# A two-block transformer: the query parts written to memory once, by chunk, and the query stack loaded by three transfers that repeat their rows

## The chip, the cores and the metric

One core of one Trainium2 chip runs the whole program in one launch. The metric is the device time of that launch in microseconds (us), smaller is better. TensorE (PE) multiplies matrices, VectorE (DVE) reduces and adds, ScalarE (ACT) applies functions and moves results out of PSUM, GpSimd (POOL) does side work, and SyncE (SP) issues nearly all transfers (DMAs) between the on-chip memory (SBUF) and the chip's main memory. 16 DMA engines carry them.

## The reference, cut to what matters

The input x has 2 sequences of 1024 tokens with 128 features. Four blocks follow, each on a layer norm of x and added to x: an attention with 16 heads of 8 features, a feed-forward net on values rounded to FP4, a stack of 6 transformer layers, and a last feed-forward net. The change lies in the attention, which runs once in the first block and once in each of the 6 layers:

```python
q = (h @ wq + bq_).reshape(Bx, Sx, H, HD).transpose(0, 2, 1, 3)      # H = 16, HD = 8, Sx = 1024
k = (h @ wk + bk_).reshape(Bx, Sx, H, HD).transpose(0, 2, 1, 3)
v = (h @ wv + bv_).reshape(Bx, Sx, H, HD).transpose(0, 2, 1, 3)
scores = jnp.einsum('bhqd,bhkd->bhqk', q, k) * scale
scores = scores * smask          # 6 layers: kept where the bits of q's and k's place do not meet
a = jax.nn.softmax(scores, axis=-1)
att = jnp.einsum('bhqk,bhkd->bhqd', a, v)
```

## The kernel before, in words

**Halves.** The work goes by halves: one sequence in one attention layer. The first attention has 2 halves (the dense stage, `A0`), the 6 layers have 12 (the sparse stage, `A1`). A half's queries and keys are 1024 tokens, in two chunks x = 0, 1 of 512.

**Stacks.** A head has only 8 features, so float32 accuracy is made by parts: a query value is split into three bf16 parts (high, middle, low), a key value too. The score is the sum over all 9 pairs of parts, done as one matmul with 72 rows (`R_PAIR` = 3 x 3 x 8). For that the queries stand in `QS` with each part i repeated for j = 0, 1, 2 (rows i, j, d), and the keys in `KS` with parts j inside each i. Ten rows of mask bits and three rows of a running maximum follow. ACT writes the high part into `PQ` or `PK` (L783), DVE or POOL make the middle and low parts, and the partition layout is changed from (d, head) to (part, d) rows through main memory: `write_parts` writes the parts of a chunk to `scq` (three copies, one for each j) and `sck` (one), `load_q` and `load_k` read stacks of 8 heads (s = 0 or 1) into `QS` and `KS`.

**Units.** A half is four units k = 0..3: head group s = k // 2, query chunk x = k % 2. Pass A (L659) makes scores with queries as weights, and DVE reduces them to the maximum of each query (L948). The maximum is split in three parts, transposed to `mt`, and `move_max` sends it with three small transfers (L1076) into three rows of `QS`. Pass B (L679) makes the scores again, keys as weights, with the maximum subtracted in the same matmul; ACT takes the exponential (L804) and PE multiplies by the values (L694). PE's first matmul of a unit in pass B waits for `m_loaded`, the landing of that unit's three rows.

**Order.** The place of every step on PE, ACT and DVE is written out by hand in slots (82 for a sparse half); pass B of a half runs from slot 36 into the next half's slot 35, beside that one's pass A. In a sparse half the units of pass A start at slots 10, 31, 49 and 70, those of pass B at slots 36, 63, 77 and 104. PE executes in that order and stops at the first wait that is not met.

**SP's queue.** SP issues in the order of `sp_half`, and also stops at the first wait. For a sparse half it is: `move_max` of the half before's unit 3; `load_q(1, 0)`; `move_max` 0; `load_k(1)`; `load_q(1, 1)`; `move_max` 1; for the next half `write_parts(0)`, the layer's weights where due, `write_parts(1)`, `load_q(0, 0)`; `move_max` 2; for the next half `load_k(0)`, `load_q(0, 1)`. ACT's queue carries the small transfers of the maxima of units 2 and 3 (`sce`, `emr`). A load waits until pass B of the half before has done with the part of the stack that it overwrites, and until the parts are written.

Of the kernel before, what the change touches and what calls it, by code (L numbers as in the profile page):

```python
# [6 lines left out]
BF16 = mybir.dt.bfloat16  # L7
# [5 lines left out]
P = 128  # L13
D = 128
B, S = 2, 1024
H, HD = 16, 8
NB = S // P
NT = B * NB
CH = 512
TC = CH // P  # L20
NC = NT // TC
CB = NC // B
VW = HD + 1
NP = 3
R_PAIR = NP * NP * HD
# [350 lines left out]
def build(nc, io):  # L376
    ctx = ExitStack()
    with ctx:
# [57 lines left out]

        pA, pB, pO, pG = psum("pA", ABANKS), psum("pB", BBANKS), psum("pO", OBANKS), psum("pG", 2)

        scq = nc.dram_tensor("scq", (B, NP, NP, P, S), BF16, kind="Internal").ap()
        sck = nc.dram_tensor("sck", (B, NP, P, S), BF16, kind="Internal").ap()  # L440
        sce = nc.dram_tensor("sce", (B, UNITS, P, MC), F32, kind="Internal").ap()

# [201 lines left out]
        def pe_half(pe, a, half, slots, ready):  # L644
            cur = a.alive(half)
            for u in range(slots):
                if cur and u in a.a_at:
                    n = a.a_at[u]
                    st = a.a[n]
                    if n == a.a_first[st.k] and st.k % 2 == 0:  # L650
                        half.wait(pe, a.stack[st.k // 2], 64, 64)
                    elif n == a.a_first[st.k]:
                        half.wait(pe, a.stack_x1[st.k // 2], 16, 16)
                    half.wait(pe, a.a_reduced, n + 1 - ABANKS, a.na)
                    for gg, r, (how, keys), at, width in st.parts:
                        for hd in range(NQ):
                            head = SH * (st.k // 2) + 2 * hd + gg
                            row = KS[0:R_A, head, :]
                            ins = pe.matmul(pA[QT * hd:QT * (hd + 1), a.a_bank(half, n), at:at + width],  # L659
                                            QS[0:R_A, r // NR, head, r % NR * QT:(r % NR + 1) * QT],  # L660
                                            row[:, keys * CH:(keys + 1) * CH] if how == "half"
                                            else allowed(row, 5, keys),
                                            start=True, stop=True, tile_position=(0, QT * hd), skip_group_check=True)
                    ins.then_inc(a.a_scored, 1)
# [38 lines left out]
        def act_job(act, a, half, name):  # L703
# [52 lines left out]
            elif kind == "v":  # L756
                hw(act, a.v_evac, x + 1, CB)
                for p in range(2):
                    src = VN[KT * p:KT * (p + 1), TC * x:TC * (x + 1), :]\
                        .rearrange("p t (r a d) -> p t r a d", a=2, d=HD)  # L760
                    for ab in range(2):
                        ins = act.activation(VDv[KT * ab:KT * (ab + 1), half.b, 2 * TC * x + p:2 * TC * (x + 1):2, :,
                                                 VW * ab:VW * ab + HD], src[:, :, :, ab, :], ACT.Copy)
                ins.then_inc(a.v_placed, 1)
            elif kind == "on":
                s, xh = divmod(x, 2)
                hw(act, a.ot_filled, x + 1, UNITS)
                act.activation(on_view(half, s, xh), ot_view(a.bank[f"ot{x}"]), ACT.Copy).then_inc(a.ot_read, 1)
            else:
                assert kind == "qk"  # L770
                k, z = n[1], 2 * x + n[1]
                src = pG[:, a.bank[name], :]
                hw(act, a.qk_filled, z + 1, 2 * CB)
                if half.off or x:
                    hw(act, a.qk_split, z - 1, 2 * CB)
                half_w = 48 if k == 0 else 16
                (half + -1).wait(act, (a.q_written, a.k_written)[k][x], half_w, half_w)
                scale = SCALE if k == 0 else 1.0
                bias = (bqs[:, 0:1] if k == 0 else cE[:, 1:2]) if a.sparse else 0.0
                if a.sparse and k == 0:  # L780
                    wait_layer(act, a.bqs, half, 1)
                act.activation(x32[:, k, :], src, ACT.Identity, scale=scale, bias=bias)
                act.activation((PQ, PK)[k][:, 0, x * CH:(x + 1) * CH], src, ACT.Identity, scale=scale, bias=bias)\  # L783
                    .then_inc(a.qk_evac, 1)
# [261 lines left out]

        def load_q(sp, a, half, s, x):
            (half + -1).wait(sp, a.b_scored, a.b_end[2 * s + x] + 1, a.nb)
            half.wait(sp, a.q_written[x], 48, 48)
            hs = slice(SH * s, SH * (s + 1))  # L1050
            q = scq[half.b].rearrange("i j (d h) t -> (i j d) h t", h=H)
            sp.dma_start(QS[0:R_PAIR, x, hs, :], q[:, hs, x * CH:(x + 1) * CH])\
                .then_inc((a.stack, a.stack_x1)[x][s], 16)

        def load_k(sp, a, half, s):
            (half + -1).wait(sp, a.b_scored, a.b_end[2 * s + 1] + 1, a.nb)
# [7 lines left out]
        def write_parts(sp, a, half, x):  # L1064
            b, ts = half.b, slice(x * CH, (x + 1) * CH)
            half.wait(sp, a.qk_split, 2 * x + 2, 2 * CB)
            for j in range(NP):
                sp.dma_start(scq[b, :, j, :, ts].rearrange("i p t -> p i t"), PQ[:, :, ts]).then_inc(a.q_written[x], 16)
            sp.dma_start(sck[b, :, :, ts].rearrange("j p t -> p j t"), PK[:, :, ts]).then_inc(a.k_written[x], 16)

        def move_max(sp, a, half, k):
# [631 lines left out]
```

## Time and profile before

| | us |
|---|---|
| median of 3 runs | 1875.08 |
| lowest, highest | 1864.85, 1877.22 |
| the profiled execution's own time | 1867.36 |
| its span (first to last instruction) | 1865.5 |
| PE busy | 1606.9 (86%) |
| DVE busy | 1392.1 (75%) |
| ACT busy | 1153.2 (62%) |
| POOL busy | 369.5 (20%) |
| packets of SP's transfers (q1), as a share of 16 engines' span | 27.4% |

A busy share is an average over stages. The dense stage runs to about 530 us, the sparse stage from about 597 to 1800 us. Engine names with a q (SPq, ACTq) are the sequencers, which issue transfers and wait. What an engine waited for is inferred from semaphores. "Issue" is idle time for which the profile shows no wait. A DMA share can be a little over 1, since a packet's time is counted from its start to its end and two can overlap.

### The profile page before, as it was taken

How to read it: one execution, taken by the hardware profiler on the slowest of the kernel's cores; microseconds unless marked ns; L12 is line 12 of the kernel's file. 1: busy time of each engine (PE TensorE's matmuls, PEld its weight loads, DVE VectorE, ACT ScalarE, POOL GpSimd, SP SyncE). 2: the span in 40 equal slices, each digit the busy share in tenths (PEclk: the TensorE clock that was granted, in tenths of full speed). 3: DMA queues.
4: the chain of work that ended last, by engine and by line, in shares of the span. 5: the costliest groups of instructions: out<-in, count | busy, mean ns of one | idle time of the engine just before them, and what ended most of it. 6: DMA issues, size and time to landing. Idle time of an engine off the chain costs nothing.

```text
span 1865.5 us, 66422 instructions
## 1 busy us (share of the span) xinstructions
PE 1606.9 (86%) x28545; PEld 905.1 (49%) x28545; DVE 1392.1 (75%) x3287; ACT 1153.2 (62%) x2046; POOL 369.5 (20%) x407
## 2 busy tenths in 40 slices
PE   2899998899866789898989889898989889888886
PEld 1233333233333355555656556566565656565553
DVE  6878889987678767776776858687777777767834
ACT  2157776677842376775666666767767667666732
POOL 2000000000011223232231313232313233222111
PEclk7569999999987699999999999999999999999988
DMA  8022102000004342425233333334233434342000
GB/s 168 13 53 83 41 3 53 2 3 12 17 11 128 104 113 56 112 55 150 55 110 69 114 79 92 80 106 95 77 90 92 114 76 103 93 107 49 6 7 17
DMA packets 153754, 130.79 MB, mean 70 GB/s; under 512 B 65029, under 2 KB 149445, under 8 KB 151445
## 3 DMA queue, kind: packets, MB, share of 16 engines
q1 hardware_dynamic: 136181, 125.75, 27.4%
q8 instruction: 225, 3.69, 0.8%
q10 hardware_dynamic: 17280, 0.79, 0.6%
q14 instruction: 68, 0.56, 0.1%
HBM read 79.25 MB, written 45.88 MB: 67 GB/s over the span
## 4 chain that ended last, share of the span: by engine, by line
PE 39%; DVE 11%; ACT 6%; issue 6%; DMA 2%; ACTq 1%; SPq 1%; POOL 0%; DVEq 0%
PE pB L679 8%; PE pO L694 7%; PE pA L659 6%; PE pG L628 5%; PE pG L638 5%; DVE mx L948 3%; ACT PB L804 3%; DMA QS<-mt 2%; DVE bst L479 1%; PE pG L572 1%; PE pG L514 1%; ACTq L1090 1%; PE pG L579 1%; ACT HT L717 1%; PE pA L1229 1%
## 5 line engine op out<-in xcount | busy, mean ns | idle before, releaser
L804 ACT ACTIVATE PB<-pB 128x512 f32<-128x512 f32 (+1 forms) x1496 | 832.1, 594 | 410.9 <-PE pB L679 373.0
L948 DVE TENSOR_REDUCE mx<-pA 128x1 f32<-128x512 f32 (+3 forms) x1000 | 645.0, 671 | 194.5 <-PE pA L659 192.0
L679 PE MATMUL pB<-QS,KS 85*32 85x256 bf16 (+3 forms) x11264 | 609.9, 284 | 60.0 <-ACT PB L804 35.6
L659 PE MATMUL pA<-KS,QS 82*32 82x256 bf16 (+2 forms) x8384 | 548.0, 312 | 83.5 <-DVE mx L948 33.8
L694 PE MATMUL pO<-PB,VD 128*32 128x128 f32 (+3 forms) x5632 | 465.9, 399 | 9.3 <-issue 6.2
L679 PEld LDWEIGHTS pB<-QS,KS 85*32 85x32 bf16 x11264 | 262.4, 96 | 346.4 <-ACT PB L804 239.7
L659 PEld LDWEIGHTS pA<-KS,QS 82*32 82x32 bf16 x8384 | 217.4, 98 | 289.8 <-DVE mx L948 113.1
L502 POOL TENSOR_TENSOR rstd<-vareps,mhalf 128x4 f32<-128x4 f32 x68 | 69.9, 1027 | 1003.0 <-DVE vareps L488 1001.9
L948 DVE TENSOR_REDUCE mxb<-pA 128x1 f32<-128x512 f32 x304 | 207.0, 681 | 10.9 <-PE pA L659 10.9
L694 PEld LDWEIGHTS pO<-PB,VD 128*32 128x32 f32 x5632 | 168.5, 112 | 43.2 <-issue 11.3
L628 PE MATMUL pG<-HT,wL 128*128 128x512 f32 x192 | 99.7, 646 | 33.0 <-ACT HT L717 30.7
L638 PE MATMUL pG<-wL,FF 128*128 128x128 f32 x768 | 91.7, 278 | 1.2 <-ACT FF L738 1.2
L638 PEld LDWEIGHTS pG<-wL,FF 128*128 128x128 f32 x768 | 87.5, 192 | 6.2 <-ACT FF L738 4.0
L738 ACT ACTIVATE FF<-pG,cL 128x512 f32<-128x512 f32 x96 | 66.0, 687 | 24.8 <-PE pG L628 23.0
L861 DVE TENSOR_TENSOR ON<-ON,pG 128x288 f32<-128x288 f32 x48 | 20.7, 449 | 78.6 <-PE pG L605 78.6
L628 PEld LDWEIGHTS pG<-HT,wL 128*128 128x128 f32 x192 | 34.4, 199 | 84.6 <-issue 47.4
L572 PE MATMUL pG<-HT,wE 128*128 128x512 f32 x112 | 68.3, 698 | 3.4 <-DVE VN L838 1.9
L514 PE MATMUL pG<-ident,N 128*128 128x128 f32 x320 | 55.1, 298 | 16.4 <-DMA rE<-in_b 8.9
L1026 POOL TENSOR_TENSOR VU<-VN 128x512 f32<-128x512 f32 x12 | 15.3, 1277 | 270.3 <-PE pG L592 270.2
L495 DVE TENSOR_SCALAR N<-N,mv,rstd 128x128 f32<-128x128 f32 x208 | 58.0, 342 | 13.6 <-POOL rstd L502 13.5
L717 ACT ACTIVATE HT<-pG 128x512 f32<-128x512 f32 x32 | 19.0, 595 | 62.4 <-PE pG L514 62.4
L514 PEld LDWEIGHTS pG<-ident,N 128*128 128x128 f32 x320 | 38.0, 150 | 36.7 <-DVE N L495 12.5
(195 smaller groups left out, 1534.9 us busy)
## 6 DMA issues: line engine op xcount, KB each, us to landing
scq<-PQ SPq DMA_DIRECT2D x84, 384.0 KB, 3.5
QS<-scq SPq DMA_DIRECT2D x56, 576.0 KB
KS<-sck SPq DMA_DIRECT2D x84, 384.0 KB
sck<-PK SPq DMA_DIRECT2D x28, 384.0 KB, 4.4
wL<-in_wL SPq DMA_DIRECT2D x6, 576.0 KB, 5.0
QS<-mt SPq DMA_DIRECT2D x168, 8.0 KB, 2.5
rE<-in_rE SPq DMA_DIRECT2D x7, 256.0 KB, 11.7
emr<-sce SPq DMA_DIRECT2D x96, 4.0 KB, 1.7
```

Source lines behind the costliest of these rows:

```text
L495: ins = v.tensor_scalar(dst[:, t, :], src[:, t, :], mv[:, t, 0:1], rstd[:, t:t + 1], ALU.subtract, ALU.mult)
L502: g.tensor_tensor(rstd[:, a], vareps[:, a], mhalf[:, a], ALU.pow).then_inc(ln.rs, 1)
L514: ins = pe.transpose(pG[:, bank, i * P:(i + 1) * P], src[:, TC * c + i, :], ident[:, :])
L572: pe.matmul(pG[:, bank, :], wE[:, n[1], :], HT[:, c * CH:(c + 1) * CH], start=True, stop=True)\
L628: pe.matmul(pG[:, bank, :], wL[:, D + n[1] * P:D + (n[1] + 1) * P], HT[:, c * CH:(c + 1) * CH], start=True, stop=True).then_inc(F1.filled, 1)
L638: ins = pe.matmul(pG[:, bank, i * P:(i + 1) * P], FF[:, x, k, i * P:(i + 1) * P], wL[:, D + HID + k * D:D + HID + (k + 1) * D], start=(k = ...
L659: ins = pe.matmul(pA[QT * hd:QT * (hd + 1), a.a_bank(half, n), at:at + width], QS[0:R_A, r // NR, head, r % NR * QT:(r % NR + 1) * QT], ro ...
L679: ins = pe.matmul(pB[32 * i:32 * (i + 1), a.b_bank(h, v), at:at + width], KS[0:R_B, head, k0:k0 + 32], allowed(QS[0:R_B, x, head, :], 3, k ...
L694: ins = pe.matmul(allowed(pO[32 * j:32 * j + 32, k % OBANKS, :], 3, kt & 7 if a.sparse else 0), VD[:, col:col + 32], PB[:, a.ring(bank)[0] ...
L738: act.activation(FF[:, x, m, :], pG[:, a.bank[name], :], ACT.Gelu, bias=cL[:, 2 + m:3 + m])\
L804: act.activation(PB[:, pos_, 0:st.cols], pB[:, a.b_bank(h, v), 0:st.cols], ACT.Exp).then_inc(a.b_exped, 1)
L948: v.tensor_reduce(dst[:, gs[0]:gs[-1] + 1, tl[0]:tl[-1] + 1:step], pA[:, a.a_bank(half, n), 0:len(gs) * len(tl) * st.width] .rearrange("p ...
```

## The change

The scratch tensor `scq` is laid out by sequence, part, chunk, and then 128 partitions x 512 tokens, with no copies for j. `write_parts` writes it with one transfer of 384 KB for each chunk in place of three. `load_q` issues three transfers, one for each part i, of 24 rows (j, d) of 4096 contiguous values (8 heads x 512 tokens, 8 KB) in place of one of 72 rows with 8 pieces of 1 KB each. The source of such a transfer is 8 rows (d), read three times by a leading dimension of step 0 (j). What PE, and ACT before it overwrites `PQ`, wait for follows the new number of transfers.

```diff
--- before.py
+++ after.py
@@ -436,7 +436,7 @@
 
         pA, pB, pO, pG = psum("pA", ABANKS), psum("pB", BBANKS), psum("pO", OBANKS), psum("pG", 2)
 
-        scq = nc.dram_tensor("scq", (B, NP, NP, P, S), BF16, kind="Internal").ap()
+        scq = nc.dram_tensor("scq", (B, NP, CB, P, CH), BF16, kind="Internal").ap()
         sck = nc.dram_tensor("sck", (B, NP, P, S), BF16, kind="Internal").ap()
         sce = nc.dram_tensor("sce", (B, UNITS, P, MC), F32, kind="Internal").ap()
 
@@ -648,9 +648,9 @@
                     n = a.a_at[u]
                     st = a.a[n]
                     if n == a.a_first[st.k] and st.k % 2 == 0:
-                        half.wait(pe, a.stack[st.k // 2], 64, 64)
+                        half.wait(pe, a.stack[st.k // 2], 96, 96)
                     elif n == a.a_first[st.k]:
-                        half.wait(pe, a.stack_x1[st.k // 2], 16, 16)
+                        half.wait(pe, a.stack_x1[st.k // 2], 48, 48)
                     half.wait(pe, a.a_reduced, n + 1 - ABANKS, a.na)
                     for gg, r, (how, keys), at, width in st.parts:
                         for hd in range(NQ):
@@ -773,8 +773,7 @@
                 hw(act, a.qk_filled, z + 1, 2 * CB)
                 if half.off or x:
                     hw(act, a.qk_split, z - 1, 2 * CB)
-                half_w = 48 if k == 0 else 16
-                (half + -1).wait(act, (a.q_written, a.k_written)[k][x], half_w, half_w)
+                (half + -1).wait(act, (a.q_written, a.k_written)[k][x], 16, 16)
                 scale = SCALE if k == 0 else 1.0
                 bias = (bqs[:, 0:1] if k == 0 else cE[:, 1:2]) if a.sparse else 0.0
                 if a.sparse and k == 0:
@@ -1046,11 +1045,13 @@
 
         def load_q(sp, a, half, s, x):
             (half + -1).wait(sp, a.b_scored, a.b_end[2 * s + x] + 1, a.nb)
-            half.wait(sp, a.q_written[x], 48, 48)
+            half.wait(sp, a.q_written[x], 16, 16)
             hs = slice(SH * s, SH * (s + 1))
-            q = scq[half.b].rearrange("i j (d h) t -> (i j d) h t", h=H)
-            sp.dma_start(QS[0:R_PAIR, x, hs, :], q[:, hs, x * CH:(x + 1) * CH])\
-                .then_inc((a.stack, a.stack_x1)[x][s], 16)
+            for i in range(NP):
+                q = scq[half.b, i, x].rearrange("(d h) t -> d (h t)", h=H)[:, SH * s * CH:SH * (s + 1) * CH]
+                sp.dma_start(QS[i * NP * HD:(i + 1) * NP * HD, x, hs, :].rearrange("p h t -> p (h t)"),
+                             q.unsqueeze(0).to_broadcast([NP, HD, SH * CH]))\
+                    .then_inc((a.stack, a.stack_x1)[x][s], 16)
 
         def load_k(sp, a, half, s):
             (half + -1).wait(sp, a.b_scored, a.b_end[2 * s + 1] + 1, a.nb)
@@ -1064,8 +1065,7 @@
         def write_parts(sp, a, half, x):
             b, ts = half.b, slice(x * CH, (x + 1) * CH)
             half.wait(sp, a.qk_split, 2 * x + 2, 2 * CB)
-            for j in range(NP):
-                sp.dma_start(scq[b, :, j, :, ts].rearrange("i p t -> p i t"), PQ[:, :, ts]).then_inc(a.q_written[x], 16)
+            sp.dma_start(scq[b, :, x].rearrange("i p t -> p i t"), PQ[:, :, ts]).then_inc(a.q_written[x], 16)
             sp.dma_start(sck[b, :, :, ts].rearrange("j p t -> p j t"), PK[:, :, ts]).then_inc(a.k_written[x], 16)
 
         def move_max(sp, a, half, k):
```

SP's queue, from `write_parts(0)` for the next half to the `move_max` of unit 3, for a half that loads no weights (`scq`, `sck`: scratch in main memory; `mt`: the maxima). Before:

```order
L1068 DMA scq<-PQ 128x3x512 x3
L1069 DMA sck<-PK 128x3x512
L1068 DMA scq<-PQ 128x3x512 x3
L1069 DMA sck<-PK 128x3x512
L1052 DMA QS<-scq 72x8x512
L1076 DMA QS<-mt 1x128x32 x3
L1062 DMA KS<-sck 24x8192 x3
L1052 DMA QS<-scq 72x8x512
L1076 DMA QS<-mt 1x128x32 x3
```

And with the change:

```order
L1068 DMA scq<-PQ 128x3x512
L1069 DMA sck<-PK 128x3x512
L1068 DMA scq<-PQ 128x3x512
L1069 DMA sck<-PK 128x3x512
L1052 DMA QS<-scq 24x1x4096 x3
L1076 DMA QS<-mt 1x128x32 x3
L1063 DMA KS<-sck 24x8192 x3
L1052 DMA QS<-scq 24x1x4096 x3
L1076 DMA QS<-mt 1x128x32 x3
```

Nothing changes places: two of three writes are gone, and a load of a query stack is three transfers. The order of instructions on PE, ACT, DVE and POOL is as before.

## Rows read from the trace of the kernel before

**Rows 1.** Page, part 1 and part 4: busy time, and the chain that ended last

```profile
PE 1606.9 (86%) x28545; PEld 905.1 (49%) x28545; DVE 1392.1 (75%) x3287; ACT 1153.2 (62%) x2046; POOL 369.5 (20%) x407
...
PE 39%; DVE 11%; ACT 6%; issue 6%; DMA 2%; ACTq 1%; SPq 1%; POOL 0%; DVEq 0%
```

**Rows 2.** Waits: engine, line, what it waited for: us in total, times, longest

```profile
PEld pB L679 <- DMA QS<-mt: 8.9, 11, 1.6
...
PE pA L659 <- DMA KS<-sck: 21.9, 1, 21.9
```

**Rows 3.** Page, part 6: transfers by tile, count, KB each, us from issue to landing

```profile
scq<-PQ SPq DMA_DIRECT2D x84, 384.0 KB, 3.5
QS<-scq SPq DMA_DIRECT2D x56, 576.0 KB
...
sck<-PK SPq DMA_DIRECT2D x28, 384.0 KB, 4.4
...
QS<-mt SPq DMA_DIRECT2D x168, 8.0 KB, 2.5
```

**Rows 4.** Timeline of SP, 1349 to 1393 us: start, duration, line, transfer, count

```profile
1349.32 2.35 SPq L1068 DMA_DIRECT2D scq<-PQ  x3
1351.71 0.59 SPq L1069 DMA_DIRECT2D sck<-PK  x1
1352.40 0.87 SPq L1052 DMA_DIRECT2D QS<-scq  x1
1354.87 2.30 SPq L1076 DMA_DIRECT2D QS<-mt  x3
1358.83 1.14 SPq L1062 DMA_DIRECT2D KS<-sck  x3
1360.07 0.31 SPq L1052 DMA_DIRECT2D QS<-scq  x1
1365.41 1.77 SPq L1076 DMA_DIRECT2D QS<-mt  x3
1380.38 0.31 SPq L1052 DMA_DIRECT2D QS<-scq  x1
1392.32 1.91 SPq L1076 DMA_DIRECT2D QS<-mt  x2
```

**Rows 5.** DMA view of 1349 to 1361 us: busy tenths and GB/s, 40 slices

```profile
DMA  0020899619999999999886788889898330079225
GB/s 0 0 55 0 307 365 369 215 48 365 355 386 379 389 386 379 379 369 297 215 205 215 242 210 181 217 177 184 171 155 125 55 80 24 11 165 328 55 109 164
```

**Rows 6.** Timeline of PE where unit 2 of pass B begins, in two halves

```profile
1358.79 0.40 PE L659 MATMUL pA<-KS,QS 82*32 82x128 bf16 x16
1360.55 0.40 PE L679 MATMUL pB<-QS,KS 85*32 85x512 bf16 x4 [1.37 <-DMA QS<-mt]
...
970.95 0.24 PE L659 MATMUL pA<-KS,QS 82*32 82x128 bf16 x3 [2.03 <-issue]
...
971.67 0.74 PE L679 MATMUL pB<-QS,KS 85*32 85x512 bf16 x4
```

**Rows 7.** Timeline of PE where unit 3 of pass B begins, same halves

```profile
993.87 0.43 PE L679 MATMUL pB<-QS,KS 85*32 85x512 bf16 x4
...
1380.58 0.43 PE L679 MATMUL pB<-QS,KS 85*32 85x512 bf16 x4
```

**Rows 8.** Windows: stretch, its length, busy of five engines, PEclk, DMA share, GB/s

```profile
995.00:997.00 2.00, 2.00 (x66) 1.60 (x57) 1.73 (x4) 1.46 (x4) 1.15 (x1) 1.00 0.75 225
213.00:217.00 4.00, 3.87 (x56) 1.28 (x48) 2.50 (x5) 2.56 (x5) 0.00 (x0) 1.00 0.82 180
1113.50:1118.50 5.00, 4.89 (x18) 1.98 (x19) 0.12 (x1) 4.21 (x6) 0.99 (x1) 1.00 0.72 164
...
1352.00:1354.00 2.00, 1.91 (x19) 1.06 (x16) 1.83 (x8) 1.03 (x3) 1.51 (x4) 1.00 1.08 378
971.40:974.80 3.40, 3.40 (x88) 2.96 (x81) 2.13 (x4) 1.57 (x3) 0.00 (x0) 0.50 0.72 164
1360.50:1363.90 3.40, 3.16 (x104) 2.02 (x104) 2.41 (x6) 2.76 (x6) 0.03 (x1) 1.00 0.81 183
```

**Rows 9.** Timeline of SP in the first 60 us

```profile
22.89 1.50 SPq L1068 DMA_DIRECT2D scq<-PQ  x3
24.43 0.81 SPq L1069 DMA_DIRECT2D sck<-PK  x1
28.89 0.34 SPq L1052 DMA_DIRECT2D QS<-scq  x1
...
38.43 1.13 SPq L1062 DMA_DIRECT2D KS<-sck  x3
```

**Rows 10.** Page, part 3: DMA queue, packets, MB, share of 16 engines

```profile
q1 hardware_dynamic: 136181, 125.75, 27.4%
q8 instruction: 225, 3.69, 0.8%
```

## The prediction, made before the changed kernel ran

> **What bounds the kernel now.** I read the page's busy times first, then the chain that ended last, then the waits by engine, then SP's timeline over one sparse half, and last the DMA view of the congested stretch in it. PE is busy 86% of the span and holds most of the chain, while DMA has only 2% of it [rows 1]. The reader is to see that bytes are not the limit: SP's queue takes 27.4% of the 16 engines' time [rows 10]. So what the change does to bytes is worth little by itself. It counts only where PE waits for a landing. The waits name two such places: `mt`, the maxima that pass B needs (8.9 us in 11 waits of weight loads), and one wait of 21.9 us for the key stack at the start [rows 2].
>
> The place to look at is therefore unit 2 of pass B, once in each sparse half that still has a next half: 11 times. [Rows 4] show SP there: at 1349.3 the writes of the second chunk, at 1352.4 the load of a query stack, at 1354.9 the three `mt` transfers that PE needs, all in one queue. [Rows 5] show the DMA engines working without a break from 1350.2 (fifth slice of 0.3 us) to about 1359.2. PE ends the work before at 1359.2 and starts unit 2 at 1360.55, 1.37 us late, waiting for `mt` [rows 6]. An `mt` transfer with nothing ahead of it lands in about 2.5 us [rows 3]; here 5.7 us pass from issue to use. So the tiny transfer waits behind the large ones.
>
> **The writes.** Two of three writes of 384 KB go, once for each chunk of 14 halves: 56 issues and 22.0 MB of 125.75 [rows 3, 10]. For the first chunk nobody waits. For the second chunk, 4 x 384 KB (three of `scq`, one of `sck`) stand ahead of the query load; at 378 GB/s [rows 8] one takes 1.04 us, so removing two frees the queue 2.1 us earlier. SP has about 1 us less to issue there (0.5 us each [rows 9]) and 0.8 us more for the two extra loads (0.38 us each, as the key loads [rows 4]); it then waits for the maxima anyway.
>
> **The query loads.** The bytes stay at 576 KB (589,824 B), in pieces of 8 KB in place of 1 KB. The question is how many of the 16 DMA engines carry them. In [rows 8] the window with a 72-row query load alone has a DMA share of 0.75, and those with 24-row key loads alone 0.82 and 0.72, where four full-height writes give 1.08, which is all 16. Twelve of 16 is 0.75, and 12 is the largest number up to 16 that divides both 72 and 24. So a transfer is dealt out by equal parts of its outermost dimension. The new query load has 24 rows as destination, but its source's outermost dimension is the 3 repeats. A part must be the same elements on both sides, and only 3 divides both. No row shows a transfer whose two sides differ in this way, so the bounds are 3 and 12 engines. I take 3, since a share in twelfths would cut a repeat of the source. And the three transfers take the same three engines: of the key loads three are out together [rows 4], and their share stays at 12 of 16.
>
> The Trainium skill says the same as a rule, and against this change: "DMA: Bandwidth & Descriptors", in the section on why a DMA increments its semaphore by 16, has the engine count as the largest number up to 16 that divides the slowest dimension of both sides, and its rules for kernel authors say that a leading zero-stride broadcast of c copies confines the whole DMA to at most c engines. By it they are the lowest-numbered three for each transfer.
>
> **The rate of one engine.** Full writes give 378 / 16 = 23.6 GB/s each [rows 8]. Key loads give only 164 / 12 = 13.7 to 180 / 12 = 15.0 [rows 8]. These are the ends. I take 23.6: the key loads put 12 engines on 24 rows, while three engines on 24 rows have eight rows each, and a query load over 72 rows already reaches 225 / 12 = 18.8, so it is the crowding on few rows that slows the keys. Three engines then carry 70.9 GB/s and a query load takes 8.3 us. At 13.7 it takes 14.3 us.
>
> The Trainium skill's page "SBUF — State Buffer" (section on the DMA port swizzle) gives four neighbouring partitions one port of 27.2 GB/s. By it 24 rows have six ports, 163 GB/s, which the 164 GB/s of the key loads agree with, and three engines on two ports each would not be held by them.
>
> **The sum for one half.** In the half of [rows 4 to 6]: bytes start at 1350.2; two writes, 0.79 MB at 378 GB/s, take 2.1 us: 1352.3. The query load fills its three engines for 8.3 us: 1360.6. `mt` is dealt over all engines (its source has 128 rows), so its share on those three stands behind the query bytes. From the last query bytes at 1359.2 to PE's start at 1360.55 is 1.35 us now; the same tail gives 1361.95, 1.4 us later than now. Eleven times: +15 us. The other ends: 14.3 us gives +7.4 us each.
>
> PE's pause there grows from 1.4 to 2.75 us. A pause of 2.03 us at the same place in another half [rows 6] is followed by a granted clock of 0.50 (1.2 GHz) from 971.4 to 974.8, where the half with the pause of 1.37 us has 1.00 (2.4 GHz) [rows 8]. Unit 2 then lasts 22.2 us (971.67 to 993.87) in place of 20.0 (1360.55 to 1380.58) [rows 6, 7]: 2.2 us for a drop. Between none and eleven halves can pay it; I take five more than now, +11 us. Elsewhere PE's wait costs in full: the next matmuls of both passes stand behind it, and the exponentials of unit 2 behind those.
>
> **Loads that are covered.** The load at 1380.38 has until the next `mt` issue at 1392.32 [rows 4]: 0.9 + 8.3 us end at 1389.6. Cover gone at 11.9 us. The load at 1360.07 follows the keys on its three engines: they have 1/12 of 1.18 MB each, 98 KB at 13.7 to 15.0 GB/s, 6.6 to 7.2 us from about 1361, then 8.3 us: 1376.5, and `mt` of unit 3 lands near 1377.9, before 1380.58 [rows 7], with 2.7 us to spare. Its own use in pass A is later still. If it grew by more, unit 3's `mt` would be the next late thing, and behind it the small `sce` transfers for which ACT waits.
>
> **Start.** The first query load leaves SP at 28.89, after the write's landing [rows 9]; with one write it leaves near 26.4 (22.9 + 3.5 [rows 3]), but then fills three engines until 26.4 + 0.9 + 8.3 = 35.6, and the second chunk's writes have a sixteenth there each, 2.1 us: landed about 39.0, where the key load left at 38.43. So +0.6 us; between -2 and +7 us by the ends above. The rest of the dense stage has twice to three times the slots for a unit and no such meeting: 0.
>
> Sum: 15 + 11 + 1 = +27, less some 3 us, since pauses without a named wait like the 2.03 us "issue" at 970.95 [rows 6] are in part overlapped by the longer wait: **+24 us on the profiled execution's 1867.4: 1891 us**. That execution is 8 us under the shown median, near the lowest run; by that median the same sum would be 1899.
>
> **Rivals.**
> - *Twelve engines after all* (the destination's 24 rows decide): the query load takes 3.3 us at 180 GB/s, the queue drains by 1355.6, before `mt` is out. `mt` then lands by its own 2.5 us, about 1358.4, and the 1.37 us pause vanishes. All such waits are 8.9 us [rows 2]; with some pauses of instruction supply like that of [rows 6], -9 to -17: 1854, faster. It decides from the point at which more than three engines carry a load: with four it would already take 6.3 us, 0.6 us less than now. For it: the key loads' 24 rows. Against: the 3 in front. Chance 0.12.
> - *The slow engine rate*, 13.7 to 18 GB/s: unit 2 is 4 to 7.4 us late (44 to 81 us in eleven halves), from 11 us of load the `mt` of unit 0 too (up to 2.3 us in 12 halves, 27), and more clock drops: 1920 to 1985. For it: the only long pieces in the trace are the key loads. Chance 0.14.
> - *Instruction supply.* The PE pause at 970.95 names no wait [rows 6], and the instruction queue moves 3.69 MB over the same engines [rows 10]. If its ring is on one of the three, a fetch stands behind a query load four times a half. Some 3 us a half on top: 1925. Against: thirteen engines become emptier, and it may be one of those. Chance 0.12.
>
> My forecast has the remaining 0.62, with its own range 1876 to 1912.
>
> **How the numbers follow.** About 1% (19 us) is what a measurement can tell from no change. Faster by more: two thirds of the first rival, 0.08. Within 1%: its other third, and a quarter of my own case (fewer clock drops, a shorter tail): 0.04 + 0.15 = 0.19, with 0.01 for the rest: 0.20. Slower: 0.72. The range leaves out the first rival at the low end and the upper half of the slow rate above: 1866 to 1945.
>
> **What would show it.** In the profile after: q1's bytes fall from 125.75 to about 104 MB; a window with a query load alone shows a DMA share near 0.19 (3 of 16) and about 70 GB/s, for about 8 us. The wait of pass B for `QS<-mt` grows from 8.9 to about 25 us or more, with more windows of half clock right behind it. A share of 0.75 in that window, or a wait for `mt` that shrinks, proves the forecast wrong; a share of 0.19 at 40 GB/s is the second rival; pauses named "issue" that grow where query loads run are the third.

## The result, and the profile after

The changed kernel takes 1912.9 us (median of 4 runs, 1902.08 to 1915.41), the kernel before 1876.15 us beside it: a ratio of 1.0191, with an interval of 1.0148 to 1.0234. It is slower, by 1.5 to 2.3%. The profiled execution took 1902.08 us, 34.7 us above the one of before, where 24 were forecast. (Run once more beside some of the experiments, it took 1915.2 us, ratio 1.022.)

Page of the kernel after, parts 1, 3, 4 and 6, which answer to [rows 1, 10, 3]:

```profile
PE 1617.6 (85%) x28545; PEld 902.1 (47%) x28545; DVE 1391.4 (73%) x3287; ACT 1152.8 (61%) x2046; POOL 369.5 (19%) x407
...
q1 hardware_dynamic: 85389, 103.73, 21.1%
q8 instruction: 225, 3.69, 0.9%
...
PE 35%; DVE 13%; ACT 6%; DMA 6%; issue 5%; ACTq 1%; SPq 1%; POOL 0%; DVEq 0%
...
QS<-scq SPq DMA_DIRECT2D x168, 192.0 KB
...
scq<-PQ SPq DMA_DIRECT2D x28, 384.0 KB, 2.7
```

The 22.0 MB of writes are gone and each engine has as many instructions as before, though PE is busy 10.7 us longer with its own. But the transfers' share of the chain of waits has grown from 2% to 6%. The waits of the kernel after (engine, line, what it waited for: us in total, times, longest) say which transfer, against [rows 2]:

```profile
ACT PB L803 <- PE pB L679: 411.6, 446, 12.5
...
DVE mx L947 <- PE pA L659: 230.1, 190, 9.1
...
PEld pB L679 <- DMA QS<-mt: 52.2, 15, 7.4
...
PEld pB L679 <- issue: 35.5, 85, 1.0
...
PE pA L659 <- DMA KS<-sck: 21.4, 1, 21.4
```

The wait of pass B for the maxima went from 8.9 to 52.2 us, and longest from 1.6 to 7.4. The same two waits of ACT and DVE for PE were 373.0 and 192.0 us in the profile before: each is 38 us longer, which fits a PE that stops. The wait for the key stack at the start is as it was.

The DMA view of one sparse half of the kernel after (1374 to 1388 us, 40 slices of 0.35 us), against [rows 5], and the query loads that are alone, in the windows view (columns as in [rows 8]):

```profile
DMA  0000089999970023321211316241131211976196
GB/s 0 0 0 0 0 307 386 363 357 357 348 144 23 23 97 140 76 117 70 94 70 70 89 71 158 86 113 70 70 117 70 117 71 71 220 151 187 47 421 140
```

```profile
1005.00:1010.00 5.00, 4.92 (x122) 3.48 (x124) 4.97 (x10) 2.95 (x6) 3.55 (x4) 1.00 0.22 85
1109.00:1115.00 6.00, 5.92 (x141) 3.74 (x130) 5.97 (x13) 3.95 (x8) 4.01 (x4) 1.00 0.21 86
1210.00:1215.00 5.00, 5.00 (x119) 3.25 (x115) 4.80 (x11) 3.15 (x6) 3.94 (x4) 1.00 0.22 85
```

Where the load ran on 12 engines at a share of 0.75 before [rows 8], the share is now 0.21 to 0.22: three engines of 16 and little else. After 2.4 us of writes (slices 6 to 12) the digits are mostly 1 to 3 for some 7 us, while 13 engines have next to nothing to carry. The bytes of the three loads in these windows take 7.9 to 8.1 us from the first to the last, by the trace's packets.

SP's timeline in the same half, which answers to [rows 4], and PE where unit 2 of pass B begins, in three halves, which answers to [rows 6]:

```profile
1374.88 0.36 SPq L1068 DMA_DIRECT2D scq<-PQ  x1
1375.29 0.49 SPq L1069 DMA_DIRECT2D sck<-PK  x1
1375.88 2.26 SPq L1052 DMA_DIRECT2D QS<-scq  x3
1380.70 1.81 SPq L1076 DMA_DIRECT2D QS<-mt  x3
1385.24 1.14 SPq L1063 DMA_DIRECT2D KS<-sck  x3
```

```profile
1183.15 0.62 PE L679 MATMUL pB<-QS,KS 85*32 85x512 bf16 x4 [2.54 <-DMA QS<-mt]
...
1288.12 0.62 PE L679 MATMUL pB<-QS,KS 85*32 85x512 bf16 x4 [7.02 <-DMA QS<-mt]
...
1387.36 0.40 PE L679 MATMUL pB<-QS,KS 85*32 85x512 bf16 x4 [1.75 <-DMA QS<-mt]
```

From the issue of the writes to PE's start it is 1387.36 - 1374.88 = 12.5 us here, where the kernel before took 11.2 (1360.55 - 1349.32). I shall call this the **lead time of unit 2**; it is the number by which the kernels below are compared. But in the half of the 7.02 us wait the writes left SP at 1271.34, and the lead time is 16.8 us. Over the eleven halves the mean was 11.4 us before (10.5 to 12.1) and is 14.45 us after (12.5 to 17.9).

The two kinds of half show apart in the chain of waits (start, duration, what). In the half of 12.5 us, and in that of 16.8 us:

```profile
1381.91 5.41 DMA QS<-mt
```

```profile
1278.18 9.90 DMA QS<-mt
```

The same piece was 3.95 us long in the kernel before (from 1356.56, third `mt` issue, same half as [rows 4]).

The clock behind the wait, in three windows of the kernel after:

```profile
1183.20:1186.40 3.20, 3.20 (x72) 2.31 (x76) 1.14 (x2) 1.22 (x3) 0.00 (x0) 0.50 0.83 179
...
1288.10:1292.30 4.20, 4.18 (x96) 3.02 (x100) 1.69 (x3) 1.79 (x3) 0.00 (x0) 0.50 0.78 131
...
1387.80:1391.20 3.40, 3.40 (x96) 2.62 (x85) 1.78 (x3) 1.79 (x3) 0.00 (x0) 0.51 0.80 169
```

PE had waited 2.54, 7.02 and 1.75 us, and then ran at half clock (1.2 GHz) for 3 to 4 us each time. From the first unit 2 of the sparse stage to its last unit 3, the granted clock is halved in nine stretches before (34 us in total) and in fourteen after (88 us). Some of them are long, and PE still waits in a part of them:

```profile
1486.80:1500.50 13.70, 8.40 (x128) 4.34 (x132) 3.89 (x13) 4.55 (x9) 0.00 (x0) 0.50 0.62 108
```

### The profile page after: what moved, and what is told of

Its sections match the earlier page's. It is cut to its first block, busy times and chain, and to the rows that moved or that the text cites. A ratio compares the mean times of both kernels' runs of the same rounds, so it can differ in the third digit from the quotient of the medians.

```text
span 1900.2 us, 66478 instructions
## 1 busy us (share of the span) xinstructions
PE 1617.6 (85%) x28545; PEld 902.1 (47%) x28545; DVE 1391.4 (73%) x3287; ACT 1152.8 (61%) x2046; POOL 369.5 (19%) x407
## 3 DMA queue, kind: packets, MB, share of 16 engines
q1 hardware_dynamic: 85389, 103.73, 21.1%
## 4 chain that ended last, share of the span: by engine, by line
PE 35%; DVE 13%; ACT 6%; DMA 6%; issue 5%; ACTq 1%; SPq 1%; POOL 0%; DVEq 0%
PE pB L679 7%; PE pO L694 6%; PE pG L628 5%; PE pA L659 5%; PE pG L638 5%; DVE mx L947 5%; DMA QS<-mt 4%; ACT PB L803 3%; DVE bst L479 1%; PE pG L572 1%; DMA emr<-sce 1%; PE pG L514 1%; ACTq L1090 1%; ACT HT L717 1%; SPq L1076 1%
## 5 line engine op out<-in xcount | busy, mean ns | idle before, releaser
L679 PEld LDWEIGHTS pB<-QS,KS 85*32 85x32 bf16 x11264 | 254.5, 97 | 387.9 <-ACT PB L803 241.9
L694 PEld LDWEIGHTS pO<-PB,VD 128*32 128x32 f32 x5632 | 163.7, 113 | 40.1 <-issue 9.3
L628 PE MATMUL pG<-HT,wL 128*128 128x512 f32 x192 | 101.7, 657 | 33.5 <-ACT HT L717 31.2
L495 DVE TENSOR_SCALAR N<-N,mv,rstd 128x128 f32<-128x128 f32 x208 | 58.0, 342 | 13.6 <-POOL rstd L502 13.5
## 6 DMA issues: line engine op xcount, KB each, us to landing
QS<-scq SPq DMA_DIRECT2D x168, 192.0 KB
```

The source lines that it names most:

```text
L495: ins = v.tensor_scalar(dst[:, t, :], src[:, t, :], mv[:, t, 0:1], rstd[:, t:t + 1], ALU.subtract, ALU.mult)
L628: pe.matmul(pG[:, bank, :], wL[:, D + n[1] * P:D + (n[1] + 1) * P], HT[:, c * CH:(c + 1) * CH], start=True, stop=True).then_inc(F1.filled, 1)
L679: ins = pe.matmul(pB[32 * i:32 * (i + 1), a.b_bank(h, v), at:at + width], KS[0:R_B, head, k0:k0 + 32], allowed(QS[0:R_B, x, head, :], 3, k ...
L694: ins = pe.matmul(allowed(pO[32 * j:32 * j + 32, k % OBANKS, :], 3, kt & 7 if a.sparse else 0), VD[:, col:col + 32], PB[:, a.ring(bank)[0] ...
```

## The experiments

All were timed in five rounds beside the kernel before, whose medians there were 1874.2 to 1878.2 us. The lead time is the mean over the eleven halves of the profiled execution, and is left out where the maxima go first. Mb is PEld's wait for `QS<-mt`, in total. The changed kernel has two profiles: lead time and Mb in its row are those of the first, of 1902.08 us; in the second, of 1924.83 us, they are 15.1 and 60.1. So a difference of 0.6 us in lead time, or of 8 us in Mb, is not one that two single profiles can tell.

| kernel | median us | ratio to before, 95% | lead time | Mb |
|---|---|---|---|---|
| before | 1876 | | 11.4 | 8.9 |
| after | 1915.2 | 1.0189 to 1.0251 | 14.45 | 52.2 |
| inner repeat | 1848.8 | 0.9855 to 0.9894 | 10.0 | 3.1 |
| inner repeat, three writes | 1872.1 | 0.9961 to 1.0016 | 12.0 | 19.4 |
| after, three writes | 1973.0 | 1.0497 to 1.0553 | 18.9 | 99.6 |
| only the first load spread | 1879.9 | 0.9986 to 1.0041 | 12.7 | 30.0 |
| all but the first load spread | 1920.5 | 1.0230 to 1.0294 | 14.25 | 51.7 |
| after, keys held back | 1896.8 | 1.0093 to 1.0163 | 13.3 | 41.1 |
| after, maxima first | 1979.0 | 1.0537 to 1.0587 | | 4.4 |
| nine adjacent loads | 1880.9 | 0.9989 to 1.0049 | 12.5 | 27.6 |
| nine loads, rows 3 apart | 1869.1 | 0.9947 to 0.9998 | 11.6 | 23.2 |
| inner repeat, maxima first | 1868.9 | 0.9930 to 0.9982 | | 3.0 |

**The changed kernel once more**, as the measure for the others.

> The changed kernel once more, beside the others on the same chip. About 1.9% slower than before (1.015 to 1.023 measured), a profiled span near 1900 us, pass B waiting about 50 us for QS<-mt.

It came to 1915.2 us, 1.9 to 2.5% over the kernel before, and 2.3 us from its first median. Its profiled execution was longer than expected (a span of 1923.0 us), with a wait of 60.1 us for `QS<-mt`.

**The repeat inside instead of outside.** Same bytes, same 8 KB pieces, same three transfers; the stack's rows become (d, j), so the source's outermost dimension is the 8 rows d and the repeat stands behind it. The key load follows that row order, which takes it from 12 to 8 engines.

```diff
-                             q.unsqueeze(0).to_broadcast([NP, HD, SH * CH]))\
+                             q.unsqueeze(1).to_broadcast([HD, NP, SH * CH]))\
...
-            k = sck[half.b].rearrange("j (d h) t -> (j d) h t", h=H)
+            k = sck[half.b].rearrange("j (d h) t -> d j (h t)", h=H)[:, :, SH * s * S:SH * (s + 1) * S]
             for i in range(NP):
-                sp.dma_start(KS[i * NP * HD:(i + 1) * NP * HD, hs, :], k[:, hs, :]).then_inc(a.stack[s], 16)
+                sp.dma_start(KS[i * NP * HD:(i + 1) * NP * HD, hs, :].rearrange("p h t -> p (h t)"), k).then_inc(a.stack[s], 16)
```

> The changed kernel, but the repeat is put inside the feature dimension: rows of a part stand as (d, j) in place of (j, d), in the query stack and in the key stack (so a key load is dealt by 8 as well). Same bytes, same number of transfers, same 8 KB pieces, same single write. Theory 1 (three engines carry a query load because the source's outermost dimension is 3): now 8 engines carry it, a query load takes 3.3 to 4 us in place of 8.1 to 8.4, the wait for QS<-mt falls from about 50 us to below 5, and the time is 1850 to 1868, under before. Theory 2 (it is the form of the loads, three transfers of 8 KB pieces where one of 1 KB pieces was, or the source being read three times): nothing changes, 1895 to 1915.

Measured: 1848.8 us, 66 us under the changed kernel, and 1.3% under the one before. Two lone loads of it, in windows (columns as in [rows 8]), and its only waits for stacks:

```profile
1082.50:1086.00 3.50, 3.50 (x90) 2.53 (x80) 3.23 (x8) 2.82 (x7) 2.97 (x3) 1.00 0.44 154
1177.50:1180.50 3.00, 3.00 (x83) 2.22 (x74) 2.83 (x6) 2.43 (x7) 2.65 (x3) 1.00 0.49 169
```

```profile
PE pA L659 <- DMA KS<-sck: 26.4, 9, 21.1
...
PEld pA L659 <- DMA KS<-sck: 9.2, 8, 2.5
```

The share is near 8 of 16, the rate about twice that of the changed kernel, and of the waits for `QS<-mt` 3.1 us are left. This version beats both the kernel before and the changed one. So with the order of two dimensions, and the key load that follows it, the sign of this change turns. (The key load is an edit of its own; more on that below.)

**The writes, with wide and with narrow loads.** Two kernels put the three writes back (copies in a scratch tensor of three; nothing reads the second and third), one on the inner repeat, one on the changed kernel.

```diff
...
-            sp.dma_start(scq[b, :, x].rearrange("i p t -> p i t"), PQ[:, :, ts]).then_inc(a.q_written[x], 16)
+            for j in range(NP):
+                sp.dma_start(scq3[j, b, :, x].rearrange("i p t -> p i t"), PQ[:, :, ts]).then_inc(a.q_written[x], 16)
```

> The kernel with the repeat inside the feature dimension (8 engines, 1849 us), with the three writes put back. It says what the saved writes are worth when the load is wide. Behind the second write: 2.1 us of bytes more ahead of the maxima of unit 2. There they landed with 1 to 2 us to spare, so about 0 to 1.5 us a half come back as a wait, and PE's pauses without a named wait return in part: +5 to +20 us, 1855 to 1870. If it stays at 1849 within 4 us, the gain over the kernel before comes from the loads' form (8 KB pieces, 24 rows) and not from the writes.

> The changed kernel with the three writes of the query parts put back (copies to three places, the loads still read one of them by the repeat). It says what the saved writes are worth. Theory 1: in each of 11 halves two more writes of 384 KB, 2.1 us, stand ahead of the query load and the maxima at unit 2, so +2.1 x 11 = +23 us over the changed kernel, near 1925 by its profile. If the saved writes are worth nothing even here (the load's start is set by something else), it is within 5 us of the changed kernel.

On the inner repeat they cost 23.3 us (1872.1 against 1848.8), 2.1 us a half for eleven halves, which is what the prediction gave them, and a little over the 5 to 20 us expected here; and with them the kernel stands at the time of before. So the rest of the change, its 8 KB pieces and the keys' form taken together, brought nothing measurable there, and the 1.3% are the writes. On the changed kernel the same writes cost 58 us (1973.0 against 1915.2), the lead time goes up by 4.5 us, and Mb nearly doubles. 2.1 us later is not all that happens to a narrow load.

**Which of the four loads.** One kernel spreads only `load_q(0, 0)`, the load that stands ahead of unit 2's maxima, into nine transfers of 8 rows; another spreads the three others.

```diff
...
+                if s == 0 and x == 0:
+                    for j in range(NP):
+                        r = (i * NP + j) * HD
+                        sp.dma_start(QS[r:r + HD, x, hs, :].rearrange("p h t -> p (h t)"), q)\
+                            .then_inc((a.stack, a.stack_x1)[x][s], 16)
+                    continue
...
```

> The changed kernel, with one of the four query loads of a half, the one ahead of the maxima of unit 2 (s = 0, x = 0), done by nine transfers of 8 rows each without a repeat (each dealt by 8 over 8 engines); the other three loads stay on three engines. If the place counts (theory 1), the wait for QS<-mt falls from about 50 us to below 15, and the time comes back to 1865 to 1885, though three quarters of the bytes still go over three engines. What can spoil it is SP: nine issues of 0.4 to 0.8 us, 3.6 to 7 us, the upper end of which would delay the maxima by 2 us. If the three-engine loads cost wherever they stand, a quarter of the loss comes back: near 1905.

> The mirror of the run before: only the load ahead of the maxima of unit 2 stays on three engines, the other three go by nine transfers of 8 rows. Theory 1: the wait for QS<-mt stays near 50 us and the time within 10 us of the changed kernel, 1900 to 1920. If the loads cost wherever they stand: near 1885.

Spreading the first alone takes back 35 us and gives the time of before, though the wait for `QS<-mt` fell only to 30.0 us and not below 15; spreading the other three takes back nothing (1920.5). That is the place. The key loads are the same in these two kernels and in the changed one, so these 35 us are the query load's. That the three others are covered is told more plainly by the waits of the kernel after, which name no wait for `QS<-scq`, and only one for `KS<-sck`, at the start.

**The keys held back.** SP waits for the landing of unit 2's maxima before it issues the next half's key load.

```diff
             if nxt:
+                if cur:
+                    half.wait(sp, a.m_loaded, 48 * 3, 48 * UNITS)
                 load_k(sp, a, half + 1, 0)
```

> The changed kernel, but SP waits for the landing of the maxima of unit 2 before it issues the key load of the next half. In the profile of the changed kernel the maxima land 12.4 to 12.8 us after the second write in five of eleven halves, as worked out in the prediction, and 13.5 to 18 in six; in the test that moved the maxima, query packets took 0.6 us in place of 0.31 while keys were in flight. Theory: the key load, which leaves at 9 to 10 us, slows the tail of the query load on the rows' ports. Then here all landings are near 12.5, the wait for QS<-mt falls by 15 to 20 us, and the keys, 2 to 3 us later, land at 22 to 23 us, still before pass A needs them at about 25: 1885 to 1900 by its profile, 10 to 20 under the changed kernel. Rival (the slow halves come from the start of the load, whose first packets take 1 us): no gain, or a loss of up to 2 us a half from later keys.

Measured: 1896.8 us, 18 us under the changed kernel. Its lead times lie between 12.2 and 14.7 us; the group above 15 us, which the changed kernel has in four of eleven halves (16.1 to 17.9 us; in its second profile seven, 15.0 to 16.9), is gone. (The group near 12.5 us, five halves in the expectation, is four in the trace.) The longest wait says so too:

```profile
PEld pB L679 <- DMA QS<-mt: 41.1, 15, 4.5
```

So a part of the loss was this: SP issues the keys 9 to 10.5 us behind the writes, while the narrow load is still on its engines and the maxima are not yet there.

The trace's single packets show more, and that the rival of the expectation (slow first packets) is half of the story. A packet of 8 KB takes 309 ns in mid-load, on three engines at a time. In the four long halves of the changed kernel the load starts badly: its first nine packets are done only 5.5 to 7.0 us after the issue of the writes, and in the seven others at 4.5 to 5.0. And in these four alone the last packets, beside the keys, take up to 0.9 us each. The second profile divides in the same way: 5.5 to 6.0 us in its seven long halves, 4.6 to 4.8 in the four others. With the keys held back late starts remain (up to 6.9 us), but no last packet is slow, and from the load's last byte to PE's start it is 0.9 to 1.7 us in every half, in place of 1.1 to 3.5. So in the changed kernel the long halves have both, a late start and the keys. What makes the first packets slow stays open.

**The maxima first.** In the changed kernel and in the inner repeat, unit 2's `move_max` goes ahead of `load_q(0, 0)`.

```diff
-                if cur:
-                    load_q(sp, a, half + 1, 0, 0)
             if cur:
                 move_max(sp, a, half, 2)
+            if nxt and cur:
+                load_q(sp, a, half + 1, 0, 0)
```

> The changed kernel with one step of SP moved: the maxima of unit 2 are sent before the query load (0, 0) of the next half, the three engines stay. Theory 1 (the maxima wait behind the query load in the queues of the same three engines): the wait at unit 2 vanishes (about 50 us of waits, 35 us of time); but the three engines then carry load, keys, load one after the other until about 35 us after the write, so the maxima of unit 3 come 1 to 2 us late in each half, and the first pass A of the next half up to 1 us late: 1870 to 1890. Rival (the transfers of the maxima themselves got slower, or PE is held by something else): 1895 to 1915.

> The inner repeat (wide loads) with the maxima of unit 2 sent ahead of the first query load instead of behind it. With loads on three engines the same edit cost 64 us, since the load ran into the key loads. If that loss came from the three engines' backlog, then with wide loads it is gone: the query load and the keys share engines evenly and the order should move the time by under 1%: 1840 to 1860, the key stack landing at most 2 us later. If putting the maxima first is bad whatever the width (rival: the load leaves later and pass A of the next half waits for it), 1870 or more.

Both fell short. The waits of the first, on narrow loads, and of the second, on wide ones:

```profile
DVE mx L947 <- PE pA L659: 291.7, 183, 18.5
...
PE pA L659 <- DMA KS<-sck: 104.9, 12, 22.6
...
PEld pA L659 <- DMA KS<-sck: 88.8, 11, 12.1
```

```profile
PE pA L659 <- DMA KS<-sck: 40.0, 10, 21.2
...
PEld pA L659 <- DMA KS<-sck: 23.2, 9, 3.5
```

The wait for `mt` nearly disappears in both (4.4 and 3.0 us are left), and comes back as a wait for the key stack. SP and PE in one half of the first:

```profile
1320.72 1.78 SPq L1076 DMA_DIRECT2D QS<-mt  x3
1322.60 2.26 SPq L1052 DMA_DIRECT2D QS<-scq  x3
1324.97 1.45 SPq L1063 DMA_DIRECT2D KS<-sck  x3
```

```profile
1346.67 0.62 PE L659 MATMUL pA<-KS,QS 82*32 82x512 bf16 x4 [5.39 <-DMA KS<-sck]
```

The keys leave 2.4 us behind the query load, and pass A of the next half gets them at 1346.7, 22 us after their issue. The load's packets take 309 ns before the keys come, and mostly 0.6 to 0.9 us beside them. In the changed kernel they leave 9.4 us behind it (1385.24 - 1375.88), and most of the load is gone from its three engines by then. The time that SP spends waiting for the maxima was not idle time. With wide loads the same order costs 20 us (1868.9 against 1848.8) instead of 64 (1979.0 against 1915.2), so two thirds of it go with the narrow loads (and the keys' form, which differs too). Where the other 20 come from was not taken further; the key wait that remains, 14 us longer than in the inner repeat, suggests the load among the keys again.

**Nine loads of eight rows, adjacent and apart.** The first spreads all query loads as above. The second does so in the row order of the inner repeat, so that the 8 rows of a transfer lie 3 apart.

```diff
...
-                sp.dma_start(QS[i * NP * HD:(i + 1) * NP * HD, x, hs, :].rearrange("p h t -> p (h t)"),
-                             q.unsqueeze(1).to_broadcast([HD, NP, SH * CH]))\
+                for j in range(NP):
+                    sp.dma_start(QS[i * NP * HD + j:(i + 1) * NP * HD:NP, x, hs, :].rearrange("p h t -> p (h t)"), q)\
...
```

> The changed kernel with every query load as nine transfers of 8 rows (one for each pair of parts), the key loads left as they are. Same bytes and 8 KB pieces, no repeated source row. It takes the spread of the query loads alone, without the other row order that the inner repeat brought to the key loads. If three engines are the cause (theory), no narrow load is left: 1850 to 1865, 50 us or more under the changed kernel, PEld's wait for QS<-mt below 30 us; what it is above the 1848.8 of the inner repeat is the price of six more issues for each load (some 2 us of SP each) and of key loads on 12 engines. If the key loads' new form was what made the inner repeat fast (rival), it stays at 1880 or above, like the kernel in which only the first load was wide.

> The row order and the key loads of the inner repeat, but each query load as nine transfers of 8 rows, whose rows lie 3 apart in the stack instead of next to each other. In the kernel with nine transfers of 8 adjacent rows the engines were as busy in a lone load as with the inner repeat (DMA share 0.46 to 0.50 against 0.44 to 0.49), but moved 71 to 79 GB/s against 154 to 169. Theory: eight engines crowd on eight adjacent rows, so spreading the same eight rows over 22 should raise the lone load to 120 GB/s or more, PEld's wait for QS<-mt falls well below the 27.6 us of the adjacent rows, and the time is 1850 to 1867 (what is over 1848.8 is six more issues for a load). Rival A: the size of the transfer or its many issues limit it, wherever the rows lie: again 70 to 85 GB/s and 1870 to 1885. Rival B: the read side (eight rows read at once) limits: the same numbers as rival A for the rate, but 1860 to 1875 through the other key loads.

The first expectation failed: 1880.9 us, no better than with one load spread. That is the time its rival had named, by which the keys' form made the inner repeat fast, so the time alone cannot turn that rival away; the rates can say what else there is. Lone loads in windows, of the adjacent kernel and then of the other (columns as in [rows 8]):

```profile
1203.00:1209.00 6.00, 6.00 (x155) 4.15 (x151) 5.96 (x12) 3.69 (x7) 4.44 (x4) 1.00 0.46 71
1305.00:1310.00 5.00, 5.00 (x115) 3.26 (x108) 5.00 (x11) 3.37 (x6) 4.45 (x4) 1.00 0.50 79
```

```profile
1183.50:1189.50 6.00, 6.00 (x162) 4.24 (x155) 5.91 (x12) 3.43 (x8) 4.44 (x4) 1.00 0.29 92
1087.50:1092.50 5.00, 5.00 (x115) 3.48 (x114) 4.78 (x10) 3.19 (x6) 4.31 (x4) 1.00 0.32 93
```

Eight engines are busy in the first (0.46 to 0.50) but move 71 to 79 GB/s, under 10 GB/s each (71 / (0.46 x 16) = 9.6); the changed kernel's three engines move 85. With the rows apart a busy engine moves 20 GB/s (92 / (0.29 x 16)), as with the inner repeat (154 / (0.44 x 16) = 22), so for the rate of an engine adjacency was the limit, and not the read of 8 rows or the size of a transfer. The 120 GB/s that I expected did not come, for a dull reason: SP needs longer to issue the nine than the engines to carry them.

```profile
1181.49 6.60 SPq L1053 DMA_DIRECT2D QS<-scq  x9
```

That is 64 KB every 0.73 us, 89 GB/s. With adjacent rows the nine are issued in less than half the time:

```profile
1200.68 3.00 SPq L1055 DMA_DIRECT2D QS<-scq  x9
```

With this, the kernel with one load spread reads differently too: its 35 us show the place, but its form was a poor one, and it is no measure of what a wide load gives. The key loads' form is not separated: it came with the inner repeat's row order, in each of the kernels that have it, and none changed it alone. So of the 66 us between the changed kernel and the inner repeat, 35 are shown to be the query load's; how the other 31 divide between its better form and the keys' is not shown.

## Why the prediction was right, and where its size was off

The direction, the cause and the place held. By its own steps:

- **Bytes, writes, start.** 103.73 MB for the 104 forecast. The writes' 2.1 us a half is what they are worth where nothing else meets them (23.3 us in eleven halves). The start was forecast at +0.6 us; the wait there is 21.4 us for 21.9 [rows 2].
- **Three engines.** Share 0.21 to 0.22 for the 0.19 forecast; the inner repeat takes it away, by changing how the two sides divide, and with it (and the keys' new form) the whole loss; without touching the keys, spreading one load takes back 35 us of it. "Twelve engines after all" has fallen. The Trainium skill's rule that a leading zero-stride broadcast confines the transfer ("DMA: Bandwidth & Descriptors", rules for kernel authors) is borne out by it.
- **The rate.** Forecast 8.3 us for a load and 70.9 GB/s for three engines; measured about 8 us alone, and 85 GB/s in mid-load, all traffic counted. The load's own packets, 8 KB in 309 ns, make 26.5 GB/s an engine, where the forecast took 23.6. The slow rate has fallen as a rival: the maxima are late, but through what meets the load, not through its rate.
- **Instruction supply.** PEld's pauses named "issue" ahead of pass B's matmuls shrank, from 43.8 us in the profile before to 35.5. Fallen.
- **Covered loads.** Right: no wait for `QS<-scq` is named, and PE's 11 waits for `QS<-mt` in the profile after are all for unit 2, so unit 3's `mt`, with 2.7 us to spare, is not late.
- **The clock.** Five more drops at 2.2 us, +11, were forecast. There are five more stretches of half clock in the sparse stage, but they are longer, 88 us in total for 34, with PE waiting in a part of them. What they cost is not measured by itself. PE's busy time for the same matmuls is 10.7 us longer, and the eleven units 2 together are 7 us longer (244.5 us before, 251.5 after).
- **The lead time is the term that was mis-sized.** "1.4 us later than now, eleven times: +15". Taken over all halves it is +3.05 us, 33.5 us in eleven. In four halves the forecast is right to 0.2 us: it gave 1361.95 - 1349.32 = 12.6, and 12.5 to 12.8 were measured. In the other seven it is 13.6 to 17.9. The working followed the load's bytes to their end, 11.3 us behind the writes, and laid the tail of [rows 6], 1.35 us, behind them; it counted nothing that could reach the three engines before the maxima did. By the packets the bytes end at 12.2 us on average and the tail is 2.3 us. Holding the keys back brings the mean lead time down to 13.3 us, which shows 1.2 us of the excess of 1.85 (14.45 - 12.6), or 1.8 of 2.5 by the second profile. It is the tail that the keys had stretched: without them it is 1.2 us, while the bytes still end at 12.1. They take 7.9 to 9.7 us there, 8.9 on average in place of 8.3, which is about the size of the rest; what is over 309 ns a packet there lies mostly in the first packets.
- **Small slips, which the sum does not use.** [Rows 5] have one slice of 0.3 us at a tenth (from 1351.4), so the engines did not work quite "without a break". The cover of the load at 1380.38 is gone at 11.0 us of load, since 0.9 of the 11.9 us go before its first byte. SP takes 2.26 us to issue the three loads, not 3 x 0.38. And of the two key windows of [rows 8] only the one of 164 GB/s agrees with the 163 set beside it; the other has 180.

With 33.5 for the lead time, 7 for the longer units 2 and a remainder of -6 that no row explains, the sparse stage is 34.6 us longer (1104.7 for 1070.1 us from the first pass A to the last), which is the whole of the difference. The forecast had 15 + 11 + 1 - 3. So the direction and the place were foreseen, and the lead time came out at more than twice its term. The median, 1912.9, lies within the range of 1866 to 1945, and just over the forecast's own range of 1876 to 1912, on the slow side, where the paragraph on covered loads had the collision's ingredients: it timed the *second* load behind the keys, but not the keys behind the first.

## What to carry to other kernels

In these kernels a transfer's width followed how its two sides divide, and a repeat put outermost made it as narrow as the repeat: look at the DMA share of a window in which it is alone, and if it is 3/16, put the repeat behind another dimension (here 66 us for the load and the key load in its row order). A narrow transfer has to be judged by what stands behind it on its own engines, small transfers that need all of them above all, and by what arrives while it lasts; a sum that ends with its bytes is too small (15 us forecast, 33.5 measured). When an edit takes bytes off a queue, measure that part alone before the part that pays for it: here the writes were worth 23 us, and their companion took 66 away.

## What the runs showed of the hardware that I had not expected

- Eight engines on eight adjacent rows of the on-chip memory are no faster than three on 24 rows (85 GB/s): 71 to 79 GB/s at a DMA share of 0.46 to 0.50, against 154 to 169 GB/s at 0.44 to 0.49 when each transfer covers 24 rows, and 20 GB/s for a busy engine when the 8 rows lie 3 apart. The Trainium skill ("SBUF — State Buffer", section on the DMA port swizzle) has four neighbouring partitions share a port; the direction agrees. By its figure of 27.2 GB/s eight adjacent rows on two ports would get an estimated 54; 71 to 79 were measured, and the measurement decides.
- SP's issue of a transfer depends on its form: 6.60 us for nine whose rows lie 3 apart, 0.73 each, against 3.00 us for nine with adjacent rows; the changed kernel's three, with their repeat, take 2.26 us.
- A busy share says little of bytes: 0.46 went with 71 GB/s, and 0.44 with 154.
- A narrow load's packets are slow at its start (0.6 to 1.7 us for the first two, in the changed kernel) and then take 309 ns each; beside the keys, with the maxima first, mostly 0.6 to 0.9 us.
